# Three more split down projections, three low parts on VectorE, one joint product for router and shared expert

## The chip, the cores and the metric

One core of one Trainium2 chip runs the whole program in one launch. The metric is the device time of one execution in microseconds. The kernel before took 72.2 us in the median of three runs (72.13 to 73.02).

The engines are named as in the profile: PE is TensorE (PEld its weight loads), ACT is ScalarE, DVE is VectorE, POOL is GpSimd and SP is SyncE, which issues almost all transfers.

## The reference, cut to what matters

The input is 4 x 32 tokens of 256 features, so T = 128 tokens, one per partition. Three layers follow one another, each on a layer norm of x and each added to x: a cross attention, a self attention whose four projections carry LoRA updates, and a mixture of experts. The last one is the one that fills the time:

```
logits = flat @ router_w.T                      # 32 experts
scores = sqrt(softplus(logits))
_, idx = top_k(scores + expert_bias, 4)
topv   = take(scores, idx);  topv /= topv.sum() + 1e-20
for every expert e:                             # all 32, weight 0 where not chosen
    g = clip(flat @ wg[e].T, -7, 7); u = clip(flat @ wu[e].T, -7, 7)
    out += p[:, e] * ((silu(g) * u) @ wd[e].T)
out += clamped_swiglu(flat, shared_gate_w, shared_up_w, shared_down_w)
```

Everything is fp32. Each expert has an inner width of 128.

## The kernel before, in words

The experts are taken in 16 pairs, and "unit n" is pair n (n = 1 to 16); unit 0 is the shared expert. In code `p` is the pair counted from 0, so unit n is p = n - 1. For each unit four engines work in turn:

- **PE**, `gate_up(n)` (L581): the product of x with gate and up weights of both experts, 512 columns, into the PSUM bank `bGU[n % 5]`. The first two units (`WHOLE` = 2) are multiplied whole in fp32 (L567). The other units are split: weights and x are each a high part (fp32r) and a low part (the rest), and high times high, high times low and low times high are added, six matmuls a unit.
- **DVE**, `clip(n)` (L955) reads that bank into `gu_clip`; **ACT**, `silu_unit(n)` (L784) writes silu back into the bank; **DVE**, `gate_h(n)` (L1009), two instructions, makes h and so frees the bank (`h_ready`).
- **PE**, `transpose_h(n)` (L593) into `bHT[n % 2]`; **ACT**, `hT_unit(n)` (L790) copies it to SBUF (as a high part for the split downs); **DVE**, `hT_low(n)` (L1022) makes its low part, for split downs only.
- **PE**, `down(n)`: for n up to `FIRST` = 5 in fp32 (L603), and for the last `LAST` = 11 units split (L614, L616).

High parts of weights are copies by ACT (`gu_high` L692 for a pair, `gu_high_chunk` L699 for half a pair, `dn_high` L797 for the down weights of a pair). Low parts are subtractions by POOL: `gu_low(p, c)` (L347), 28 of them, and `dn_low(i)` (L353), 11 of them, where i = 0 is the first split down. POOL does them in a written order: the pairs' gate-up parts one after the other, from p = 12 on (`BETWEEN`) each pair followed by one `dn_low`, and the remaining `dn_low` at the end. The weights come in through eight raw slots and go to seven slots of parts (`SLOTS`), so that ACT's copy for pair p waits until `gate_up` of the unit seven earlier is done.

The order on PE is written out: gate_up(1), the router product (L630) within it, the shared product (L636), gate_up(2) to (5), the transposes of units 0 and 1, and then for n = 2 to 16: gate_up(n + 4), transpose_h(n), down(n - 2) (at n = 2 the shared down, L652). gate_up(n) waits for h_ready of unit n - 5, whose bank it takes. ACT's order in turn n is silu_unit(n + 2), gu_high(10 + n), hT_unit(n), dn_high; DVE's is gate_h(n), clip(n + 2), hT_low(n - 2).

The route from the logits to the expert weights is a chain of small instructions of ACT and DVE (L763 to L998) which starts with an absolute value on ACT (L763). That one waits for the logits and for the third layer norm's 1/sqrt(var) from POOL (`inverse_sqrt(2)`, L329). The DVE clips of units 0 and 1 stand within the chain, those of units 2 and 3 behind gate_h(1).

Earlier, in the self attention, POOL's `inverse_sqrt(1)` (L329) stands behind gu_low(2, 0). It releases the broadcast product L514, then DVE's `xnT` (L922, both halves of the features in one instruction), then the projections of keys and queries (L381).

Of the kernel before, what the change touches and what calls it, by code (L numbers as in the profile page):

```python
# [40 lines left out]
LAST = 11  # L41
BETWEEN = 12
# [13 lines left out]
SMALL = ROUTER + DC * E  # L56
# [14 lines left out]
def build(nc, x, consts, mask, small, ctx_kv, x_wq, lora, rows, attn_w, shared_w, moe_w, out):  # L71
    with ExitStack() as ctx:
# [22 lines left out]
        shared_sb = sb("shared_sb", [128, DC * 2 * I + D])  # L95
# [78 lines left out]
        bLogits, bShared = bXT1, bXT0  # L174
# [4 lines left out]
        bGU = (bP[0][:, 0], bP[0][:, 1], bP[1][:, 0], bP[1][:, 1], bE)  # L179
# [74 lines left out]
        dn_lo_ready = sem("dn_lo_ready")  # L254
        gu_hi_ready = sem("gu_hi_ready")
# [13 lines left out]
        def _(sp):  # L269
# [42 lines left out]
        def _(pool):  # L312
# [43 lines left out]
            for p in range(WHOLE, PAIRS):  # L356
                for c in range(DC):
                    if (p, c) == (WHOLE, 1):
                        inverse_sqrt(1)
# [3 lines left out]
                if p >= BETWEEN:  # L363
                    dn_low(p - BETWEEN)
            for i in range(PAIRS - BETWEEN, LAST):
                dn_low(i)

        @block.tensor
        def _(pe):
# [8 lines left out]
            def project_T(which, c, w, x_t, done, biased=False):  # L378

                for k in range(DC):  # L380
                    last = nc.tensor.matmul(bP[c][:, which, 0:T], w[:, k, c * 128:(c + 1) * 128], x_t[:, k, :],  # L381
# [142 lines left out]
            pe.wait_ge(xn_ready, 1)  # L524
            project_T(0, 0, aw[0], xnT, k_psum, biased=True)
# [70 lines left out]
            def down(n):  # L596
# [49 lines left out]
            for n in range(2, PAIRS + 1):  # L646
# [13 lines left out]
        def _(act):  # L660
# [102 lines left out]
            nc.scalar.activation(abs_logits[:], bLogits[:, 0:E], ACT.Abs, scale=rstd[:, 2:3]).then_inc(abs_ready, 1)  # L763
# [36 lines left out]
            gu_high_chunk(WHOLE + 7, 0)  # L800
            silu_unit(0)
# [20 lines left out]
        def _(dve):  # L822
# [99 lines left out]
            nc.vector.tensor_tensor(xnT[:], xcT[:], bRB.unsqueeze(1).to_broadcast([128, DC, T]), ALU.mult  # L922
# [180 lines left out]
```

## Time and profile before

| | |
|---|---|
| median of 3 runs | 72.2 us |
| time of the profiled execution | 72.16 us |
| its span | 70.3 us |
| busy: PE, ACT, DVE, POOL | 65.7, 46.0, 46.9, 54.0 us |
| granted clock of PE | 0.997 of full |
| transfers | 15.75 MB, done by some 46 us |

The span runs from the first to the last instruction seen by the profile; the rest of the 72.16 us lies around it. Busy time says how full an engine is; the chain that ended last says which engine the end waited for.

### The profile page before, as it was taken

The page shows a single profiled execution, that of the slowest core. Times are in us where ns is not written, and L with a number is a line of the kernel's source. Part 1 is how long each engine was busy: PE and PEld are TensorE (multiplying, and loading weights), DVE is VectorE, ACT ScalarE, POOL GpSimd, SP SyncE. Part 2 cuts the span into 40 slices and gives each one's busy share as a digit, 9 for nine tenths or more (in the row PEclk, how much of TensorE's full clock was granted, in tenths as well). Part 3 has the DMA queues.
Part 4 walks back from the last instruction along what each step waited for, and adds up shares of the span by engine and source line. Part 5 has one row for each costly group of instructions (what it writes and reads, how often), then busy time and mean ns, then how long its engine had stood idle before and what let it go on. Part 6 is the DMA issues. An engine that isn't in the chain of part 4 may idle for free.

```text
span 70.3 us, 1581 instructions
## 1 busy us (share of the span) xinstructions
PE 65.7 (93%) x544; PEld 49.2 (70%) x546; DVE 46.9 (67%) x132; ACT 46.0 (65%) x101; POOL 54.0 (77%) x59
## 2 busy tenths in 40 slices
PE   5999998998998999999999999999999999999940
PEld 2347565787864486648787878888887888788830
DVE  0058489584779536599999907758995887697440
ACT  0604547669988665678989399999968852275220
POOL 6430005499999994999799999999999999999000
PEclk9999999999999999999999999999999999999998
DMA  0899999999999999999999997100000000000002
GB/s 0 261 282 304 343 424 390 235 332 422 429 410 408 389 403 400 403 374 347 384 415 394 396 389 274 54 6 0 0 9 0 0 0 0 0 0 0 5 0 75
DMA packets 6343, 15.75 MB, mean 224 GB/s; under 512 B 704, under 2 KB 1472, under 8 KB 6336
## 3 DMA queue, kind: packets, MB, share of 16 engines
q1 hardware_dynamic: 6048, 15.39, 59.7%
q10 hardware_dynamic: 288, 0.27, 1.1%
q8 instruction: 4, 0.07, 0.4%
q14 instruction: 3, 0.02, 0.1%
HBM read 15.52 MB, written 0.13 MB: 223 GB/s over the span
## 4 chain that ended last, share of the span: by engine, by line
PE 82%; DVE 7%; ACT 4%; POOL 3%; issue 1%
PE bP L581 22%; PE bY L614 7%; PE bY L603 6%; PE bE L444 6%; PE bE L581 6%; PE bXT L593 5%; PE bP L567 5%; PE bP L381 4%; PE bY L616 3%; PE bP L408 2%; DVE shifted L851 2%; POOL gu_w L347 2%; DVE row_max L849 2%; PE bXT L437 1%; ACT probs L669 1%
## 5 line engine op out<-in xcount | busy, mean ns | idle before, releaser
L347 POOL TENSOR_TENSOR gu_w<-gu_raw,gu_w 128x512 fp32r<-128x512 f32 x28 | 35.1, 1287 | 1.4 <-ACT gu_w L699 1.4
L581 PE MATMUL bP<-gu_w,xnT_parts 128*128 128x512 f32 x66 | 18.7, 418 | 0.0
L581 PEld LDWEIGHTS bP<-gu_w,xnT_parts 128*128 128x128 f32 x66 | 12.2, 189 | 3.0 <-issue 0.5
L1009 DVE SCALAR_TENSOR_TENSOR h<-gu_clip,gate,bP 128x128 f32<-128x128 f32 x26 | 7.8, 344 | 5.3 <-ACT bP L784 5.3
L955 DVE TENSOR_SCALAR gu_clip<-bP,clip_at 128x512 f32<-128x512 f32 x13 | 10.4, 806 | 1.1 <-PE bP L581 1.1
L692 ACT ACTIVATE gu_w<-gu_raw 128x1024 fp32r<-128x1024 f32 x9 | 9.4, 1048 | 1.1 <-issue 1.1
L353 POOL TENSOR_TENSOR gu_w<-dn_w,gu_w 128x512 fp32r<-128x512 f32 x8 | 10.0, 1309 | 0.0
L790 ACT ACTIVATE hT_parts<-bXT 128x256 fp32r<-128x256 f32 x11 | 4.2, 384 | 6.4 <-PE bXT L593 6.4
L784 ACT ACTIVATE bP<-gu_clip,rstd 128x256 f32<-128x256 f32 x13 | 6.2, 473 | 0.2 <-DVE gu_clip L955 0.2
L593 PE MATMUL bXT<-consts_sb,h 128*128 128x128 f32 x33 | 6.2, 271 | 0.0
L337 POOL TENSOR_TENSOR aw_sb<-aw_sb,lora_v 128x256 f32<-128x256 f32 x2 | 1.4, 727 | 6.1 <-DMA aw_sb<-attn_w_dram 6.1
L699 ACT ACTIVATE gu_w<-gu_raw 128x512 fp32r<-128x512 f32 x10 | 5.9, 620 | 0.2 <-PE bP L581 0.2
L593 PEld LDWEIGHTS bXT<-consts_sb,h 128*128 128x128 f32 x33 | 4.4, 140 | 1.9 <-DVE h L1009 0.2
L614 PE MATMUL bY<-gu_w,hT_parts 128*128 128x512 f32 x14 | 5.7, 434 | 0.0
L444 PE MATMUL bE<-const-bfloat16-1.0 128*128 128x512 bf16 x12 | 5.0, 566 | 0.8 <-PEq L1096 0.8
L1022 DVE TENSOR_TENSOR hT_parts<-bXT,hT_parts 128x256 fp32r<-128x256 f32 x11 | 4.6, 418 | 1.0 <-ACT hT_parts L790 1.0
L603 PE MATMUL bY<-dn_w,hT 128*128 128x256 f32 x20 | 5.1, 380 | 0.0
L581 PE MATMUL bE<-gu_w,xnT_parts 128*128 128x512 f32 x18 | 4.9, 407 | 0.0
L797 ACT ACTIVATE gu_w<-dn_w 128x512 fp32r<-128x512 f32 x8 | 4.6, 628 | 0.0
L329 POOL TENSOR_TENSOR rstd<-var_eps,inv_sqrt_power 128x1 f32<-128x1 f32 x3 | 1.8, 598 | 2.9 <-DVE var_eps L836 2.9
L567 PE MATMUL bP<-gu_raw,xfT 128*128 128x512 f32 x8 | 4.0, 603 | 0.0
L616 PE MATMUL bY<-gu_w,hT_parts 128*128 128x256 f32 x14 | 3.9, 282 | 0.0
(162 smaller groups left out, 124.3 us busy)
## 6 DMA issues: line engine op xcount, KB each, us to landing
gu_raw<-moe_w_dram SPq DMA_DIRECT2D x16, 512.0 KB, 9.7
dn_w<-moe_w_dram SPq DMA_DIRECT2D x16, 256.0 KB, 9.7
aw_sb<-attn_w_dram SPq DMA_DIRECT2D x2, 512.0 KB, 7.0
shared_sb<-shared_w_dram SPq DMA_DIRECT2D x1, 384.0 KB, 14.5
small_sb<-small_dram SPq DMA_DIRECT2D x1, 370.0 KB, 6.9
xwq_sb<-x_wq_dram SPq DMA_DIRECT2D x1, 256.0 KB, 3.5
lora_sb<-lora_dram SPq DMA_DIRECT2D x1, 256.0 KB, 4.3
ctx_sb<-ctx_kv_dram ACTq DMA_DIRECT2D x1, 192.0 KB, 3.1
```

What stands on the lines that cost most here:

```text
L347: nc.gpsimd.tensor_tensor(gu_w[:, gu_slot(p), 1, cols], gu_raw[:, raw_slot(p), cols], gu_w[:, gu_slot(p), 0, cols], ALU.subtract).then_inc ...
L353: nc.gpsimd.tensor_tensor(dn_parts(i)[:, 1], dn_w[:, at:at + 2 * D], dn_parts(i)[:, 0], ALU.subtract).then_inc(dn_lo_ready, 1)
L444: nc.tensor.matmul(bank, ones, ones_wide, start=True, stop=True, skip_group_check=True)
L567: return nc.tensor.matmul(bGU[n % 5][:, 0:GU], xfT[:, k, :], gu_raw[:, raw_slot(n - 1), k * GU:(k + 1) * GU], start=(k == 0), stop=(k == D ...
L581: last = nc.tensor.matmul(bGU[n % 5][:, 0:GU], xnT_parts[:, a, k, :], gu_w[:, gu_slot(n - 1), w, k * GU:(k + 1) * GU], start=(k == 0 and a ...
L593: last = nc.tensor.transpose(bHT[n % 2][:, e * T:(e + 1) * T], h[:, n % 4, e, :], ident)
L603: last = nc.tensor.matmul(bY[:, 0:D], hT[:, n % 3, e, :], dn_w[:, at:at + D], start=False, stop=False, skip_group_check=True)
L614: nc.tensor.matmul(bY.rearrange("p (w n) -> p w n", w=2), hT_parts[:, n % 3, 0, e, :], parts, start=False, stop=False, skip_group_check=True)
L692: nc.scalar.activation(gu_w[:, gu_slot(p), 0], gu_raw[:, raw_slot(p)], ACT.Copy).then_inc(gu_hi_ready, DC)
L784: nc.scalar.activation(dst, gu_clip[:, n % 4, 0:width, 0, :], ACT.Silu, scale=rstd[:, 2:3]).then_inc(silu_ready, 1)
L955: nc.vector.tensor_scalar(gu_clip[:, n % 4, 0:width], bank[:, 0:width * 2 * I], clip_at[:, 0:1], clip_at[:, 1:2], ALU.min, ALU.max).then_i ...
L1009: last = nc.vector.scalar_tensor_tensor(h[:, n % 4, e], gu_clip[:, n % 4, e, 1, :], weight_e, bank[:, e * 2 * I:e * 2 * I + I], ALU.mult, ...
```

## The change

- `LAST` becomes 14, so `FIRST` is 2: units 3, 4 and 5 have split downs too, 14 in all.
- The low parts of the first three split downs (`STAGED` = 3) are made by DVE: ACT copies the down weights whole into the PSUM bank bE (`dn_stage`), and DVE subtracts the high part from that. POOL makes the other 11. `BETWEEN` becomes 14: POOL makes dn_low(3) behind pair 14, dn_low(4) behind pair 15, and the rest at the end.
- The bank bE is given up by gate_up after unit 4. From unit 6 on four banks are used in turn, and from unit 9 on gate_up(n) waits for h_ready of unit n - 4.
- ACT's order in turn n: silu_unit(n + 2), then (n = 2 to 4) dn_high and dn_stage, hT_unit(n), gu_high(10 + n). dn_stage(0) waits for h of unit 4, each later one for DVE's previous low part.
- Router weights stand behind the shared gate and up weights, in one product of 288 columns, done before the second half of gate_up(1). `gu_ready` counts one less.
- gu_low(2, 0) is made in two halves of 256 columns, with `inverse_sqrt(1)` between them.
- `xnT` is made in two instructions, one for each chunk, and the first projection waits for each chunk by itself.

```diff
-LAST = 11
-BETWEEN = 12
+LAST = 14
+STAGED = 3
+BETWEEN = 14
...
+        bStage = bE
+
+        def bGU(n):
+
+            if n < 6:
+                return (bP[0][:, 0], bP[0][:, 1], bP[1][:, 0], bP[1][:, 1], bE)[n % 5]
+            return (bP[0][:, 1], bP[1][:, 0], bP[1][:, 1], bP[0][:, 0])[(n - 6) % 4]
...
-            for p in range(WHOLE, PAIRS):
+            for half in range(2):
+                cols = slice(half * GU // 2, (half + 1) * GU // 2)
+                pool.wait_ge(gu_hi_ready, 1)
+                low = nc.gpsimd.tensor_tensor(gu_w[:, gu_slot(WHOLE), 1, cols], gu_raw[:, raw_slot(WHOLE), cols],
+                                              gu_w[:, gu_slot(WHOLE), 0, cols], ALU.subtract)
+                if half == 0:
+                    inverse_sqrt(1)
+            low.then_inc(gu_lo_ready[0], 1)
+            gu_low(WHOLE, 1)
+            for p in range(WHOLE + 1, PAIRS):
                 for c in range(DC):
-                    if (p, c) == (WHOLE, 1):
-                        inverse_sqrt(1)
                     if (p, c) == (WHOLE + 5, 0):
                         inverse_sqrt(2)
                     gu_low(p, c)
                 if p >= BETWEEN:
-                    dn_low(p - BETWEEN)
-            for i in range(PAIRS - BETWEEN, LAST):
+                    dn_low(STAGED + p - BETWEEN)
+            for i in range(STAGED + PAIRS - BETWEEN, LAST):
                 dn_low(i)
...
                 if n > 5:
-                    pe.wait_ge(h_ready, n - 4)
+                    pe.wait_ge(h_ready, n - 4 if n < 9 else n - 3)
...
-                    pe.wait_ge(dn_lo_ready, i + 1)
+                    if i < STAGED:
+                        pe.wait_ge(dn_lo_dve_ready, i + 1)
+                    else:
+                        pe.wait_ge(dn_lo_ready, i - STAGED + 1)
...
             pe.wait_ge(xf1_ready, 1)
+            pe.wait_ge(ld["shared"], 16)
             for k in range(DC):
-                last = nc.tensor.matmul(bLogits[:, 0:E], xfT[:, k, :], small_sb[:, ROUTER + k * E:ROUTER + (k + 1) * E],
+                last = nc.tensor.matmul(bShared[:, 0:SHARED], xfT[:, k, :], shared_sb[:, k * SHARED:(k + 1) * SHARED],
                                         start=(k == 0), stop=(k == DC - 1))
             last.then_inc(logits_ready, 1)
             gate_up_whole(1, 1).then_inc(gu_ready, 1)
-            pe.wait_ge(ld["shared"], 16)
-            for k in range(DC):
-                last = nc.tensor.matmul(bShared[:, 0:2 * I], xfT[:, k, :], shared_sb[:, k * 2 * I:(k + 1) * 2 * I],
-                                        start=(k == 0), stop=(k == DC - 1))
-            last.then_inc(gu_ready, 1)
...
+            def dn_stage(i):
+
+                if i:
+                    act.wait_ge(dn_lo_dve_ready, i)
+                else:
+                    act.wait_ge(h_ready, 5)
+                at = (FIRST + i) * 2 * D
+                nc.scalar.activation(bStage[:], dn_w[:, at:at + 2 * D], ACT.Copy).then_inc(stage_ready, 1)
...
                 if n + 2 <= PAIRS:
                     silu_unit(n + 2)
+                if 0 <= n - 2 < STAGED:
+                    dn_high(n - 2)
+                    dn_stage(n - 2)
+                hT_unit(n)
                 if EARLY + n < PAIRS:
                     gu_high(EARLY + n)
-                hT_unit(n)
-                if 0 <= n - 2 < UNITS:
-                    dn_high(n - 2)
...
-            nc.vector.tensor_tensor(xnT[:], xcT[:], bRB.unsqueeze(1).to_broadcast([128, DC, T]), ALU.mult
-                                    ).then_inc(xn_ready, 1)
+            for c in range(DC):
+                nc.vector.tensor_tensor(xnT[:, c], xcT[:, c], bRB, ALU.mult).then_inc(xn_ready, 1)
...
+            def dn_low(i):
+
+                dve.wait_ge(stage_ready, i + 1)
+                dve.wait_ge(dn_hi_ready, i + 1)
+                nc.vector.tensor_tensor(dn_parts(i)[:, 1], bStage[:], dn_parts(i)[:, 0], ALU.subtract
+                                        ).then_inc(dn_lo_dve_ready, 1)
+
             for n in range(2, PAIRS + 1):
                 gate_h(n)
                 if n + 2 <= PAIRS:
                     clip(n + 2)
+                if 0 <= n - 4 < STAGED:
+                    dn_low(n - 4)
                 if n - 2 > FIRST:
                     hT_low(n - 2)
```

## Rows read from the trace of the kernel before

**Rows 1.** Page, busy us of each engine, its share of the span, instructions.
```profile
PE 65.7 (93%) x544; PEld 49.2 (70%) x546; DVE 46.9 (67%) x132; ACT 46.0 (65%) x101; POOL 54.0 (77%) x59
```

**Rows 2.** Chain that ended last, in order: start us, us, what.
```profile
27.86 0.36 PE bXT L630 x4
...
29.17 0.86 PE bXT L636 x4
...
37.68 0.22 PE bXT L593 x2
...
43.31 1.40 PE bE L581 x6
...
44.93 0.86 PE bY L603 x4
...
54.73 0.24 PE bY L614
...
55.44 1.41 PE bE L581 x6
...
66.73 0.13 PE bY L616
```

**Rows 3.** Timeline, 15 to 17 us: start us, us, engine, line, operation, [idle before].
```profile
15.37 0.56 POOL L329 TENSOR_TENSOR rstd<-var_eps,inv_sqrt_power 128x1 f32<-128x1 f32 x1
15.44 0.42 DVE L868 SCALAR_TENSOR_TENSOR aw_sb<-bE,aw_sb 128x256 f32<-128x256 f32 x1
...
15.88 0.29 DVE L918 COPY xcT<-bXT 128x128 f32<-128x128 f32 x1
...
16.56 0.42 DVE L922 TENSOR_TENSOR xnT<-xcT,bE 128x256 f32<-128x256 f32 x1 [0.39 <-PE bE L514]
```

**Rows 4.** Timeline, start of the route's chain.
```profile
27.96 0.68 POOL L329 TENSOR_TENSOR rstd<-var_eps,inv_sqrt_power 128x1 f32<-128x1 f32 x1 [0.96 <-DVE var_eps L836]
...
28.67 0.29 ACT L763 ACTIVATE abs_logits<-bXT,rstd 128x32 f32<-128x32 f32 x1 [1.17 <-POOL rstd L329]
```

**Rows 5.** Timeline, all engines: h of unit 2, silu of unit 3, loads for unit 2's transposes.
```profile
36.80 0.60 DVE L1009 SCALAR_TENSOR_TENSOR h<-gu_clip,gate,bP 128x128 f32<-128x128 f32 x2
36.92 0.48 ACT L784 ACTIVATE bP<-gu_clip,rstd 128x256 f32<-128x256 f32 x1
...
37.45 0.21 PEld L593 LDWEIGHTS bXT<-consts_sb,h 128*128 128x128 f32 x2 [0.21 <-DVE h L1009]
```

**Rows 6.** Timeline of ACT, from pair 12's copy to pair 13's.
```profile
40.10 1.06 ACT L692 ACTIVATE gu_w<-gu_raw 128x1024 fp32r<-128x1024 f32 x1 [1.09 <-issue]
41.07 0.37 ACT L790 ACTIVATE hT<-bXT 128x256 f32<-128x256 f32 x1
41.33 0.62 ACT L797 ACTIVATE dn_first<-dn_w 128x512 fp32r<-128x512 f32 x1
41.85 0.47 ACT L784 ACTIVATE bP<-gu_clip,rstd 128x256 f32<-128x256 f32 x1
42.25 1.04 ACT L692 ACTIVATE gu_w<-gu_raw 128x1024 fp32r<-128x1024 f32 x1
```

**Rows 7.** Timeline of DVE: clip of unit 5, h of unit 4, clip of unit 6.
```profile
38.55 0.81 DVE L955 TENSOR_SCALAR gu_clip<-bP,clip_at 128x512 f32<-128x512 f32 x1
39.27 0.60 DVE L1009 SCALAR_TENSOR_TENSOR h<-gu_clip,gate,bE 128x128 f32<-128x128 f32 x2
39.78 0.81 DVE L955 TENSOR_SCALAR gu_clip<-bP,clip_at 128x512 f32<-128x512 f32 x1
```

**Rows 8.** Groups on DVE by form: busy us, mean ns of one | idle before.
```profile
L844 DVE TENSOR_TENSOR k_heads<-bP,consts_sb 128x512 f32<-128x512 f32 x4 | 2.7, 689 | 1.7 <-PE bP L381 1.0 <-PE bP L455 0.7
...
L1022 DVE TENSOR_TENSOR hT_parts<-bXT,hT_parts 128x256 fp32r<-128x256 f32 x11 | 4.6, 418 | 1.0 <-ACT hT_parts L790 1.0
```

**Rows 9.** Timeline of POOL: its unbroken runs of low parts.
```profile
33.95 10.05 POOL L347 TENSOR_TENSOR gu_w<-gu_raw,gu_w 128x512 fp32r<-128x512 f32 x8 [0.36 <-ACT gu_w L699]
...
55.17 10.04 POOL L353 TENSOR_TENSOR gu_w<-dn_w,gu_w 128x512 fp32r<-128x512 f32 x8
```

More of the change, by code:

```diff
@@ L55 @@
 ROUTER = EBIAS + E
-SMALL = ROUTER + DC * E
+SMALL = ROUTER
+SHARED = 2 * I + E
 def gu_slot(p):
@@ L376, in merge_lora, with project_T @@
                                  start=True, stop=True).then_inc(lora_psum[m], 1)
-            def project_T(which, c, w, x_t, done, biased=False):
+            def project_T(which, c, w, x_t, done, biased=False, chunks_ready=None):
                 for k in range(DC):
+                    if chunks_ready is not None:
+                        pe.wait_ge(chunks_ready, k + 1)
                     last = nc.tensor.matmul(bP[c][:, which, 0:T], w[:, k, c * 128:(c + 1) * 128], x_t[:, k, :],
@@ L522, in values_part @@
                 return values(bE, lambda k: xnT[:, k, :], lambda k: aw[2][:, k, :], DC, batches)
-            pe.wait_ge(xn_ready, 1)
-            project_T(0, 0, aw[0], xnT, k_psum, biased=True)
+            project_T(0, 0, aw[0], xnT, k_psum, biased=True, chunks_ready=xn_ready)
             project_T(1, 0, aw[1], xnT, q_psum)
@@ L580, in gate_up @@
                         for a, w in HI_LO:
-                            last = nc.tensor.matmul(bGU[n % 5][:, 0:GU], xnT_parts[:, a, k, :],
+                            last = nc.tensor.matmul(bGU(n)[:, 0:GU], xnT_parts[:, a, k, :],
                                                     gu_w[:, gu_slot(n - 1), w, k * GU:(k + 1) * GU],
@@ L651, in _ @@
                     pe.wait_ge(ln_step, 3)
-                    nc.tensor.matmul(bY[:, 0:D], hT[:, 0, 0, :], shared_sb[:, DC * 2 * I:], start=False, stop=False,
+                    nc.tensor.matmul(bY[:, 0:D], hT[:, 0, 0, :], shared_sb[:, DC * SHARED:], start=False, stop=False,
                                      skip_group_check=True).then_inc(y_done, 1)
@@ L762, in _ @@
             act.wait_ge(logits_ready, 1)
-            nc.scalar.activation(abs_logits[:], bLogits[:, 0:E], ACT.Abs, scale=rstd[:, 2:3]).then_inc(abs_ready, 1)
+            nc.scalar.activation(abs_logits[:], bLogits, ACT.Abs, scale=rstd[:, 2:3]).then_inc(abs_ready, 1)
             act.wait_ge(abs_ready, 1)
@@ L781, in silu_unit @@
                 width = 2 if n else 1
-                bank = bGU[n % 5] if n else bShared
+                bank = bGU(n) if n else bShared
                 dst = bank[:, 0:width * 2 * I].rearrange("p (e w i) -> p e w i", e=width, w=2)[:, :, 0, :]
@@ L950, in clip @@
                 width = 2 if n else 1
-                bank = bGU[n % 5] if n else bShared
-                dve.wait_ge(gu_ready, max(2, n + 1))
+                bank = bGU(n) if n else bShared
+                if n:
+                    dve.wait_ge(gu_ready, n)
+                else:
+                    dve.wait_ge(logits_ready, 1)
                 if n >= 4:
@@ L966, in _ @@
             dve.wait_ge(abs_ready, 1)
-            step(nc.vector.tensor_scalar(logits_n, bLogits[:, 0:E], rstd[:, 2:3], None, ALU.mult))
+            step(nc.vector.tensor_scalar(logits_n, bLogits, rstd[:, 2:3], None, ALU.mult))
             dve.wait_ge(one_plus_ready, 1)
@@ L1005, in gate_h @@
                     dve.wait_ge(hT_psum, n - 3)
-                bank = bGU[n % 5] if n else bShared
+                bank = bGU(n) if n else bShared
                 for e in range(2 if n else 1):
@@ L1070 @@
     small[:, EBIAS:EBIAS + E] = v["L0_ffn_expert_bias"][None, :]
-    small[:, ROUTER:] = chunked(v["L0_ffn_router_w"]).reshape(128, DC * E)
     w_kv = v["L0_xattn_Wkv_expand"].T
```

20 lines of the change are left out of this document (11 added, 9 removed).

## The prediction

> **What bounds the kernel now.** I read the busy times first. PE is busy for 93% of the span, POOL for 77%, ACT and DVE for two thirds [rows 1]. A share says little over stages, so I took the chain that ended last, in order of time. From the first row of [rows 2] to the last, 27.86 to 66.86 us, it holds PE pieces alone, each beginning where the one before ends. So in that stretch every instruction taken from PE is worth its full length, as long as no wait takes its place. The next question is how near the next wait is. For that I read the timeline around PE's products that depend on h, then ACT's and POOL's queues. Two places are near. The weight loads for the transposes of unit 2 already sat idle for 0.21 us, until DVE ended h of unit 2 at 36.80 + 0.60 = 37.40 us [rows 5]; PE's stream hid that. And POOL makes low parts from 33.95 us, at 10.05 / 8 = 1.256 us each, to 55.17 + 10.04 = 65.21 us [rows 9]; the last split down begins where the chain's last row ends, at 66.86 us [rows 2].
>
> **Early edits, one by one.**
> - Router product: PE loses a piece of 0.36 us; the shared product of 0.86 us grows from 256 to 288 columns, 0.86 x 288 / 256 = 0.97 [rows 2]. Gain 0.25 us.
> - xnT in chunks: one instruction of 0.42 us becomes two; the nearest row with 128 columns takes 0.29 us [rows 3]. The first projection starts 0.13 us earlier, and its first chunk lasts about as long as DVE needs for the second. Gain 0.13.
> - POOL's half low part: 1/sqrt(var) now ends at 15.37 + 0.56 = 15.93 us. Earlier by some 0.2 us, it would no longer be what L514 waits for: DVE's merge ends at 15.44 + 0.42 = 15.86 us [rows 3]. Gain at most 0.07. One more POOL instruction delays later low parts by about half a microsecond; POOL idles 0.96 us before 27.96 us [rows 4], which covers it.
>
> Together PE is 0.45 us earlier at gate_up(2).
>
> **Where that goes.** The route's chain starts with L763 at 28.67 us, when POOL's 1/sqrt(var) ends at 28.64 us [rows 4]. After the change that would be 0.2 us earlier, but the logits now come with the joint product: the router piece ended at 28.22 us, the joint one ends at 27.86 - 0.20 + 0.97 = 28.63 us [rows 2]. So the chain starts when it did. From there DVE is busy almost throughout, up to h of unit 2, which again ends at 37.40 us. The transposes of unit 2 can't start their load before 37.44 us, against 37.45 now [rows 5]. The 0.45 us are spent waiting there. I count the early edits at 0, with bounds of -0.45 (the chain keeps pace) and +0.1 (the logits come later than worked out).
>
> **Three more split downs.** An fp32 down takes 0.86 us [rows 2], a split one 55.44 - 54.73 = 0.71 us [rows 2]. Three of them: -0.45 us, on the path.
>
> **What feeds them, on ACT.** From the starts in [rows 6] each instruction holds ACT for: silu 0.40, copy of a pair 0.97, hT 0.26, down copy 0.52, together 2.15 us a unit, less than the 44.93 + 0.86 - 43.31 = 2.48 us that PE takes [rows 2]. The staging copy has no row. The nearest is the down copy of the same 512 columns, SBUF to SBUF, 0.52 apart and 0.62 long [rows 6]. Lower bound: what 512 more columns cost a copy, 0.97 - 0.52 = 0.45. Upper bound: silu, which writes PSUM, holds ACT 0.14 us longer than hT for as many columns, 256; twice that on 0.52 is 0.80. I take 0.54, near the same shape. Three units then take 2.69 us each, above PE's 2.48.
>
> Walking the new order from silu(3) at 36.92 us [rows 5]: hT(1), pair 11's copy 37.58, silu(4) 38.55, down copy 38.95. dn_stage(0) waits for h of unit 4, which ends at 39.87 us [rows 7], and starts at 39.91. Behind it stand hT(2) and pair 12's copy, which starts at 40.71 us and not at 40.10, where its transfer let it start before [rows 6]. Then, by the same steps: silu(5) 41.68, silu(6) 44.37, pair 14's copy ends 47.14, and the down copy for i = 3 ends at 49.97 us.
>
> The Trainium skill (ScalarE: Activation LUTs, "Step-by-step: what each stage is for") says that ScalarE reaches PSUM faster than SBUF. No row here has the same operation with both targets; by that rule the staging copy lies near its lower bound, and the sum would be +0.3 instead of +0.5 us.
>
> **On DVE.** Three subtractions of 512 columns, one operand in PSUM: 0.69 us each, as L844 [rows 8], and three more hT_low of 0.42. DVE had waited for ACT's silu in these turns, so they fit: the starts are h of unit 5 at 42.19, clip 42.70, subtraction 43.42, hT_low(3) 44.05 (an h holds DVE for 39.78 - 39.27 = 0.51, a clip for 39.27 - 38.55 = 0.72 [rows 7]). hT_low(3) ends at 44.47, in time for PE (43.31 + 1.40 = 44.71 [rows 2]). hT_low(4) ends at 47.16, and with 0.04 for the semaphore and 0.14 for the weight load PE starts at 47.34 instead of 47.07: +0.27 us. The transposes need it because they overwrite its bank. h of units 6 and 7, for which gate_up(10) and (11) wait now that there are four banks, are late by 0.02 and 0.08 us.
>
> **On POOL.** It still makes eleven low parts of downs. But it now waits for ACT's copies: pair 12 at 41.81, pair 13 at 44.49, pair 14 at 47.18, then dn_low(3) at 50.01. Behind that stand two low parts of pair 15 and then dn_low(4), which starts at 50.01 + 3 x 1.256 = 53.78 and ends at 55.07 us. down(7) needs it. It begins at 55.07 + 0.04 + 0.14 = 55.25 us; now it begins at 54.73 [rows 2]. PE would be ready at 54.66, so it waits for 0.59 us. After that POOL gains on PE: its last low part ends near 66.4 us, 0.8 us before it is needed.
>
> **The sum.** 0 (early) - 0.45 + 0.27 + 0.02 + 0.08 + 0.59 = +0.51 us, which is 55.25 - 54.73. On the profiled execution: 72.16 + 0.5 = 72.7 us. That execution stands 0.04 us below the median of 72.2, which I neglect. With the copy at 0.45 the sum is +0.3 (72.5), at 0.80 +1.4 (73.5).
>
> **Rivals.**
> - *The downs' saving stays, the new waits don't.* The early gain is lost at unit 2 all the same. 72.16 - 0.45 = 71.7 us. For it: PE's wait at down(7) is the end of a chain of four small delays, and the instructions in between could be spaced closer. Against it: even with POOL held up only at pair 12, dn_low(4) ends near 54.4 us, and ACT has no idle time left to catch up.
> - *The route's chain comes forward too*, so that 0.45 us early and 0.45 us late both remain: 71.3 us. For it: the joint product might end sooner than by its columns. Against: the idle weight load [rows 5] and the unchanged instructions on DVE.
> - *DVE and POOL block each other*, and it is slower. Each of DVE's three subtractions would hold POOL for its 0.69 us; 2.07 us of delay reach dn_low(4), and down(7) starts at 57.3: 74.7 us. It decides as soon as POOL loses about 0.9 us beyond what I have, for then the total passes 2%. Against it: hT_low, also with one operand in PSUM, takes 0.42 us beside a busy POOL [rows 8], and POOL's parts keep their 1.256 us then [rows 9].
>
> The Trainium skill (SBUF — State Buffer, "SBUF: two separate sides") says that DVE and GpSimd take an exclusive lock when the DVE instruction has two SBUF inputs and GpSimd reads SBUF. By it the staging in PSUM avoids the lock, and this rival falls.
>
> That the change does not do what it says has one form: POOL keeps 11 low parts of downs, so it is relieved of nothing; that is in the forecast.
>
> **Chances.** Forecast 0.62, saving of the downs alone 0.20, both savings 0.08, blocking 0.07, something else 0.03. The range of 71.5 to 73.4 us takes in the first rival and nearly all of the forecast's bounds. 2% is 1.44 us, about what a measurement of this kernel can tell from no change: below 70.8 lies almost nothing, above 73.6 the blocking case. Faster 0.03, same 0.90, slower 0.07.
>
> **What would show it.** L763 starts at 28.6 to 28.7 us although gate_up(2) ends 0.45 us earlier, and PE's loads for the transposes of unit 2 are idle for some 0.6 us. L797 and the staging copy stand ahead of hT in three turns, ACT has no gap between 40 and 50 us. POOL has gaps before pairs 12, 13 and 14 and before dn_low(3). The chain that ended last passes through POOL's dn_low(4) to the down of unit 7 at about 55.2 us. The forecast is wrong if PE has no gap between 44 and 56 us, if h of unit 2 ends before 37.2 us, or if POOL's parts or DVE's subtractions last longer than 1.3 and 0.7 us.

## The result, and the profile after

The changed kernel took 72.87 us (median of 21 runs) beside 72.23 us for the kernel before (21 runs, taken in turn on one chip). The ratio is 1.0092 [1.0065, 1.0119]: 0.66 us more, a real difference, within the 2% that I called no change, and close to the forecast of 72.7. Medians are of all executions; the ratios leave out the slow ones, more than 1.5% above the fastest of their kernel, and the traces of e3, e9, e10 and e12 below are of such (73.91, 73.87, 72.65 and 72.26 us). The profiled execution took 73.24 us, its span 71.4 us; that of before took 72.16 us. So the two traces differ by 1.08 us, 0.4 us more than the ratio says; two waits for transfers that this execution had and most others had not are shown below.

The busy times, page of the changed kernel, against [rows 1]:

```profile
PE 65.5 (92%) x542; PEld 47.8 (67%) x542; DVE 49.9 (70%) x139; ACT 49.1 (69%) x107; POOL 54.5 (76%) x60
```

PE does 0.2 us less in a span that is 1.1 us longer, so PE waited more. ACT and DVE each have 3 us more work, POOL 0.5.

**Two intervals.** The first part of the kernel differs from one execution to the next: the statistics of the third norm start anywhere from 26.20 to 28.86 us in the fourteen traces. To compare kernels all the same, I cut the time at three instructions of DVE: those statistics, the start of h of unit 2, written h(2), and the last addition. Timeline of DVE, kernel before:

```profile
27.04 0.43 DVE L943 BATCH_NORM_STATS2 stats<-bY 128x6 f32<-128x256 f32 x1 [0.52 <-PE bY L433]
...
29.81 0.37 DVE L971 RECIPROCAL bXT<-bXT 128x32 f32<-128x32 f32 x1
...
67.77 0.42 DVE L1037 TENSOR_TENSOR x_sb<-bP,xc 128x256 f32<-128x256 f32 x1
```

and of the changed kernel:

```profile
26.89 0.43 DVE L972 BATCH_NORM_STATS2 stats<-bY 128x6 f32<-128x256 f32 x1 [0.52 <-PE bY L454]
...
30.13 0.37 DVE L1003 RECIPROCAL bXT<-bXT 128x32 f32<-128x32 f32 x1 [0.24 <-DVE bXT L1002]
...
37.13 0.59 DVE L1041 SCALAR_TENSOR_TENSOR h<-gu_clip,gate,bP 128x128 f32<-128x128 f32 x2
...
40.86 0.69 DVE L1061 TENSOR_TENSOR dn_first<-bE,dn_first 128x512 fp32r<-128x512 f32 x1
...
68.87 0.42 DVE L1078 TENSOR_TENSOR x_sb<-bP,xc 128x256 f32<-128x256 f32 x1
```

Interval A, statistics to h(2): 36.80 - 27.04 = 9.76 us before, 37.13 - 26.89 = 10.24 after. Interval B, h(2) to the last addition: 30.97 before, 31.74 after. With the statistics 0.15 us earlier, -0.15 + 0.48 + 0.77 = +1.10 us.

Without one wait the statistics would have come earlier still. From DVE's first read of the key product (`k_heads`) to the statistics it is 27.04 - 17.79 = 9.25 us before, and 9.25 to 9.28 us in eleven of the other traces, but 26.89 - 17.13 = 9.76 us in this one (and 9.84 in e10). ACT's timeline of the changed kernel has a copy there that waited for its transfer, ahead of the queries:

```profile
17.93 0.63 ACT L718 ACTIVATE gu_w<-gu_raw 128x512 fp32r<-128x512 f32 x1 [0.80 <-DMA gu_raw<-moe_w_dram]
```

**Interval B: where PE waited.** The starts of gate_up in PE's timeline show it, for an unhindered unit has a fixed length. Kernel before:

```profile
37.98 1.75 PE L581 MATMUL bP<-gu_w,xnT_parts 128*128 128x512 f32 x6
...
50.43 1.76 PE L581 MATMUL bP<-gu_w,xnT_parts 128*128 128x512 f32 x6
...
52.95 1.56 PE L581 MATMUL bP<-gu_w,xnT_parts 128*128 128x512 f32 x6
...
55.28 1.10 PE L581 MATMUL bE<-gu_w,xnT_parts 128*128 128x512 f32 x4
```

Five units with an fp32 down take (50.43 - 37.98) / 5 = 2.49 us each, the first with a split down 2.52 (it still begins behind an fp32 one), the next 2.33. The changed kernel:

```profile
38.30 1.76 PE L601 MATMUL bP<-gu_w,xnT_parts 128*128 128x512 f32 x6
...
43.34 1.67 PE L601 MATMUL bP<-gu_w,xnT_parts 128*128 128x512 f32 x6
...
46.04 1.63 PE L601 MATMUL bP<-gu_w,xnT_parts 128*128 128x512 f32 x6
...
48.70 1.62 PE L601 MATMUL bP<-gu_w,xnT_parts 128*128 128x512 f32 x6
...
51.08 1.57 PE L601 MATMUL bP<-gu_w,xnT_parts 128*128 128x512 f32 x6
...
53.41 1.57 PE L601 MATMUL bP<-gu_w,xnT_parts 128*128 128x512 f32 x6
...
56.39 1.56 PE L601 MATMUL bP<-gu_w,xnT_parts 128*128 128x512 f32 x6
```

The steps are 2.70, 2.66, 2.38, 2.33, 2.98 us, where without waits they would be 2.52 and then 2.33. So PE waited 0.18, 0.33, 0.05, 0 and 0.65 us. The two steps ahead of them, 43.34 - 38.30 = 5.04 us, are 0.06 longer than twice 2.49: gate_up(9), which now takes the bank of unit 5, started right behind h(5). Waits of 1.27 us less the three downs' saving of 0.48 make 0.79, against the 0.77 of interval B. PE's weight loads show what it waited for:

```profile
37.77 0.20 PEld L613 LDWEIGHTS bXT<-consts_sb,h 128*128 128x128 f32 x2 [0.55 <-DVE h L1041]
...
45.05 0.20 PEld L613 LDWEIGHTS bXT<-consts_sb,h 128*128 128x128 f32 x2 [0.48 <-issue]
...
47.71 0.20 PEld L613 LDWEIGHTS bXT<-consts_sb,h 128*128 128x128 f32 x2 [0.48 <-issue]
...
55.58 0.19 PEld L637 LDWEIGHTS bY<-gu_w,hT_parts 128*128 128x128 f32 x1 [0.62 <-POOL gu_w L365]
```

The first answers to the load in [rows 5]: idle 0.55 us instead of 0.21. The next two are the transposes of units 5 and 6, whose bank DVE has to have read first. The profile names no releaser, but they start 0.11 and 0.12 us behind the ends of hT_low(3) and hT_low(4) in DVE's timeline, and h and ACT's copy of that bank were done 1 us and more ahead of the loads:

```profile
44.53 0.41 DVE L1054 TENSOR_TENSOR hT_parts<-bXT,hT_parts 128x256 fp32r<-128x256 f32 x1
...
47.18 0.41 DVE L1054 TENSOR_TENSOR hT_parts<-bXT,hT_parts 128x256 fp32r<-128x256 f32 x1
```

The last is down(7), for POOL. POOL's timeline answers to [rows 9]:

```profile
34.05 7.54 POOL L359 TENSOR_TENSOR gu_w<-gu_raw,gu_w 128x512 fp32r<-128x512 f32 x6 [0.59 <-ACT gu_w L718]
42.37 7.86 POOL L359 TENSOR_TENSOR gu_w<-gu_raw,gu_w 128x512 fp32r<-128x512 f32 x6 [0.78 <-ACT gu_w L711]
50.48 1.29 POOL L365 TENSOR_TENSOR gu_w<-dn_w,gu_w 128x512 fp32r<-128x512 f32 x1 [0.26 <-ACT gu_w L816]
...
54.25 12.56 POOL L365 TENSOR_TENSOR gu_w<-dn_w,gu_w 128x512 fp32r<-128x512 f32 x10
```

The unbroken run that began at 33.95 in [rows 9] is now cut at pairs 12, 13, 14 and before dn_low(3): by 0.78, by 0.32 together for pairs 13 and 14 (7.86 - 7.54, six parts each), and by 0.26 us, 1.36 us in all. dn_low(4) starts at 54.25 us, and the chain that ended last passes through it:

```profile
50.48 1.29 POOL gu_w L365
51.77 2.51 POOL gu_w L359 x2
54.28 1.25 POOL gu_w L365
55.58 0.50 PE bY L637
```

From there to 67.97 us it holds PE alone. ACT's timeline, against [rows 6]:

```profile
40.22 0.60 ACT L827 ACTIVATE bE<-dn_w 128x512 f32<-128x512 f32 x1 [0.34 <-DVE h L1041]
40.76 0.37 ACT L809 ACTIVATE hT<-bXT 128x256 f32<-128x256 f32 x1
41.23 1.06 ACT L711 ACTIVATE gu_w<-gu_raw 128x1024 fp32r<-128x1024 f32 x1
42.19 0.46 ACT L803 ACTIVATE bP<-gu_clip,rstd 128x256 f32<-128x256 f32 x1
...
43.11 0.58 ACT L827 ACTIVATE bE<-dn_w 128x512 f32<-128x512 f32 x1
43.63 0.36 ACT L809 ACTIVATE hT_parts<-bXT 128x256 fp32r<-128x256 f32 x1
...
44.84 0.46 ACT L803 ACTIVATE bP<-gu_clip,rstd 128x256 f32<-128x256 f32 x1
```

The staging copy holds ACT for 40.76 - 40.22 = 0.54 us, the next for 0.52, and silu(5) to silu(6) takes 44.84 - 42.19 = 2.65 us (walked: 2.69). hT to pair 12's copy takes 0.47 us instead of 0.26. The copy waits for two things only, its transfer and gate_up(6), which was done before 38.30 us, so here it was the transfer: ACT's queue stood at that wait (L710) for 0.95 us, and for 0.04 us in a second trace of this kernel (e11). That is the 0.2 us by which interval B exceeds that of e11.

### The profile page after: what moved, and what is told of

The parts are those of the page before. It is cut to its first block, busy times and chain, and to the rows that moved or that the text cites. A ratio compares the mean times of both kernels' runs of the same rounds, so it can differ in the third digit from the quotient of the medians.

```text
span 71.4 us, 1596 instructions
## 1 busy us (share of the span) xinstructions
PE 65.5 (92%) x542; PEld 47.8 (67%) x542; DVE 49.9 (70%) x139; ACT 49.1 (69%) x107; POOL 54.5 (76%) x60
## 4 chain that ended last, share of the span: by engine, by line
DMA 30%; PE 25%; POOL 13%; ACT 12%; SPq 8%; DVE 5%; issue 3%; ACTq 0%
DMA gu_raw<-moe_w_dram 30%; POOL gu_w L359 9%; PE bY L637 6%; PE bP L601 6%; SPq L285 4%; POOL gu_w L365 4%; PE bY L639 3%; ACT gu_w L711 2%; PE bXT L613 2%; SPq L293 2%; ACT bP L803 2%; ACT hT_parts L809 2%; PE bP L429 2%; ACT bE L827 2%; PE bXT L458 1%
## 5 line engine op out<-in xcount | busy, mean ns | idle before, releaser
L359 POOL TENSOR_TENSOR gu_w<-gu_raw,gu_w 128x512 fp32r<-128x512 f32 x27 | 33.9, 1285 | 1.6 <-ACT gu_w L711 0.8
L601 PE MATMUL bP<-gu_w,xnT_parts 128*128 128x512 f32 x78 | 21.4, 410 | 0.0
L601 PEld LDWEIGHTS bP<-gu_w,xnT_parts 128*128 128x128 f32 x78 | 14.0, 188 | 3.6 <-issue 0.5
L365 POOL TENSOR_TENSOR gu_w<-dn_w,gu_w 128x512 fp32r<-128x512 f32 x11 | 13.8, 1296 | 0.3 <-ACT gu_w L816 0.3
L987 DVE TENSOR_SCALAR gu_clip<-bP,clip_at 128x512 f32<-128x512 f32 x15 | 12.0, 804 | 0.5 <-PE bP L601 0.5
L1041 DVE SCALAR_TENSOR_TENSOR h<-gu_clip,gate,bP 128x128 f32<-128x128 f32 x30 | 9.0, 343 | 3.8 <-ACT bP L803 3.7
L637 PE MATMUL bY<-gu_w,hT_parts 128*128 128x512 f32 x20 | 8.2, 436 | 0.4 <-POOL gu_w L365 0.4
L816 ACT ACTIVATE gu_w<-dn_w 128x512 fp32r<-128x512 f32 x11 | 6.4, 630 | 0.0
L639 PE MATMUL bY<-gu_w,hT_parts 128*128 128x256 f32 x20 | 5.6, 281 | 0.0
L637 PEld LDWEIGHTS bY<-gu_w,hT_parts 128*128 128x128 f32 x20 | 3.8, 188 | 1.1 <-POOL gu_w L365 0.6
L639 PEld LDWEIGHTS bY<-gu_w,hT_parts 128*128 128x128 f32 x20 | 3.8, 189 | 0.0
```

Of the source, the lines that this page charges most:

```text
L359: nc.gpsimd.tensor_tensor(gu_w[:, gu_slot(p), 1, cols], gu_raw[:, raw_slot(p), cols], gu_w[:, gu_slot(p), 0, cols], ALU.subtract).then_inc ...
L365: nc.gpsimd.tensor_tensor(dn_parts(i)[:, 1], dn_w[:, at:at + 2 * D], dn_parts(i)[:, 0], ALU.subtract).then_inc(dn_lo_ready, 1)
L601: last = nc.tensor.matmul(bGU(n)[:, 0:GU], xnT_parts[:, a, k, :], gu_w[:, gu_slot(n - 1), w, k * GU:(k + 1) * GU], start=(k == 0 and a == ...
L637: nc.tensor.matmul(bY.rearrange("p (w n) -> p w n", w=2), hT_parts[:, n % 3, 0, e, :], parts, start=False, stop=False, skip_group_check=True)
L639: last = nc.tensor.matmul(bY[:, 0:D], hT_parts[:, n % 3, 1, e, :], parts[:, 0], start=False, stop=False, skip_group_check=True)
L816: nc.scalar.activation(dn_parts(i)[:, 0], dn_w[:, p * 2 * D:(p + 1) * 2 * D], ACT.Copy).then_inc(dn_hi_ready, 1)
```

## The experiments

Each kernel was compared with the kernel before on the same chip, e1 to e4 on one, e5 to e8 on a second, e9 to e12 on a third. A and B are the two intervals, in us, from each kernel's trace; A + B leaves out what happens ahead of the statistics. e5, e6, e8, e9 and e10 leave out parts of the route and don't compute the reference.

| kernel | A | B | A + B | ratio |
|---|---|---|---|---|
| before | 9.76 | 30.97 | 40.73 | |
| changed | 10.24 | 31.74 | 41.98 | 1.0092 [1.0065, 1.0119] |
| e1_pool_order | 10.24 | 30.89 | 41.13 | 1.0041 [0.9993, 1.0088] |
| e2_early_only | 10.24 | 30.92 | 41.16 | 1.0022 [0.998, 1.0064] |
| e3_late_only | 9.97 | 31.53 | 41.50 | 1.0125 [1.005, 1.0199] |
| e4_no_stage | 10.28 | 31.80 | 42.08 | 1.0214 [1.014, 1.0287] |
| e5_before_short | 9.58 | 31.06 | 40.64 | 1.003 [0.9982, 1.0077] |
| e6_early_short | 9.86 | 30.92 | 40.78 | 1.0018 [0.9968, 1.0067] |
| e7_spread | 10.23 | 30.48 | 40.71 | 1.0001 [0.996, 1.0042] |
| e8_spread_short | 9.82 | 30.36 | 40.18 | 0.9897 [0.9852, 0.9943] |
| e9_before_fast | 9.16 | 31.46 | 40.62 | 1.0006 [0.9959, 1.0052] |
| e10_early_fast | 9.82 | 31.68 | 41.50 | 1.0008 [0.9951, 1.0064] |
| e11_after_again | 10.23 | 31.53 | 41.76 | 1.0127 [1.0051, 1.0202] |
| e12_spread_router | 9.98 | 30.36 | 40.34 | 0.9938 [0.9884, 0.9992] |

### e1: is it POOL's order?

```
-                if p >= BETWEEN:
-                    dn_low(STAGED + p - BETWEEN)
-            for i in range(STAGED + PAIRS - BETWEEN, LAST):
+                if p == BETWEEN:
+                    dn_low(STAGED)
+                    dn_low(STAGED + 1)
+            for i in range(STAGED + 2, LAST):
```

> The changed kernel with one difference: POOL makes dn_low(3) and dn_low(4) both behind pair 14, ahead of pair 15. Theory (down(7) waits for dn_low(4), which stands behind two low parts of pair 15): dn_low(4) ends two parts, 2.5 us, earlier, PE's wait at down(7) goes, and the time falls by 0.6 us against the changed kernel, to about that of the kernel before (within 0.2 us). Rival (the wait is only where PE's lateness shows, which comes from the transfers of the gate-up weights and ACT's queue): the time stays as that of the changed kernel, +0.6 us.

Measured: 1.0041. POOL's timeline has both parts together, ahead of pair 15:

```profile
49.95 2.54 POOL L365 TENSOR_TENSOR gu_w<-dn_w,gu_w 128x512 fp32r<-128x512 f32 x2 [0.24 <-ACT gu_w L817]
```

PE has no wait at down(7): gate_up(7) to gate_up(14) takes 17.23 us (before 17.30, changed 18.09, e11 17.86), and B is 0.64 us under e11's. So the wait goes as soon as the two parts of pair 15 no longer stand ahead of dn_low(4), though ACT's copies are as late as in the changed kernel. That doesn't clear ACT: the order costs something only because POOL had already lost 1.36 us to those copies. Without these, by my estimate, dn_low(4) ends at 55.54 - 1.36 = 54.18 us in the old order, and down(7) could not start its loads before 55.58 - 0.62 = 54.96. By that the wait needed both. Against the kernel before, e1 is at +0.30 us [-0.05, +0.63], and A + B at +0.40, where I had expected at most 0.2: what is left is interval A.

### e2 and e3: the two halves of the change

e2 keeps the joint router product, xnT in chunks and the half low parts, and takes back the late part; e3 the reverse.

```
e2:  -LAST = 14  +LAST = 11     -STAGED = 3  +STAGED = 0     -BETWEEN = 14  +BETWEEN = 12
     five banks for gate_up as before; pe.wait_ge(h_ready, n - 4)
e3:  -SHARED = 2 * I + E  +SHARED = 2 * I     router product by itself, in bXT1
     no halves of pair 2's low part; xnT in one instruction
```

> The kernel before with the early edits alone: joint product of router and shared expert, gu_low(2, 0) in two halves, xnT in two chunks. 11 split downs and five banks as before. Theory (the 0.45 us that PE gains by gate_up(2) are spent waiting for h of unit 2): same time as before, -0.1 to +0.1 us. Rival (the gain is kept): -0.45 us.

> The changed kernel without the early edits: router product by itself, gu_low(2, 0) and xnT whole. Theory (the end is set by POOL's dn_low(4), which the early edits don't reach): same time as the changed kernel, +0.5 to +0.7 us against before. Rival (the joint product, which holds up the logits, is what costs): about -0.3 to 0 us against before.

e2 measured 1.0022, that is +0.16 us with an interval of 0.3 on either side: no gain is seen, and the -0.45 us of the rival is excluded. The weight loads of PE for the transposes of unit 2 are idle as in the changed kernel:

```profile
37.38 0.20 PEld L611 LDWEIGHTS bXT<-consts_sb,h 128*128 128x128 f32 x2 [0.55 <-DVE h L1038]
```

e3 measured 1.0125, +0.9 us [+0.4, +1.4]: the late part alone costs about as much as the whole. PE's timeline has the wait at down(7):

```profile
56.23 0.50 PE L630 MATMUL bY<-gu_w,hT_parts 128*128 128x512 f32 x1 [0.40 <-POOL gu_w L365]
```

B is 30.97 + 0.56, where the walk said +0.51.

### e4: what the staging in PSUM buys

```
-                    dn_high(n - 2)
-                    dn_stage(n - 2)
+                    dn_high(n - 2)
 ...
-                nc.vector.tensor_tensor(dn_parts(i)[:, 1], bStage[:], dn_parts(i)[:, 0], ALU.subtract
+                nc.vector.tensor_tensor(dn_parts(i)[:, 1], dn_w[:, at:at + 2 * D], dn_parts(i)[:, 0], ALU.subtract
```

> The changed kernel without the three staging copies: DVE subtracts the high part from the down weights in SBUF, so both its operands lie in SBUF. Theory (the three copies of 0.54 us on ACT are what delays silu and POOL's copies): ACT's queue is 1.6 us shorter, no wait arises at units 5 to 7, -0.5 us against before, if DVE and POOL don't block each other. Rival (DVE and POOL block each other when DVE reads two operands from SBUF): each of DVE's three subtractions lasts up to 1.3 us longer than 0.69, or POOL's part beside it does, and the time is that of before or above it.

Measured: 1.0214, slower than the changed kernel though ACT has three copies less. By how much is open: 0.9 us by this ratio and 1.0092, 0.6 us by this one and e11's 1.0127, 0.1 and 0.3 us by A + B. DVE's timeline:

```profile
41.38 1.31 DVE L1060 TENSOR_TENSOR dn_first<-dn_w,dn_first 128x512 fp32r<-128x512 f32 x1
...
43.86 1.78 DVE L1060 TENSOR_TENSOR dn_first<-dn_w,dn_first 128x512 fp32r<-128x512 f32 x1
...
47.13 1.46 DVE L1060 TENSOR_TENSOR dn_first<-dn_w,dn_first 128x512 fp32r<-128x512 f32 x1
```

and POOL's:

```profile
34.60 16.40 POOL L359 TENSOR_TENSOR gu_w<-gu_raw,gu_w 128x512 fp32r<-128x512 f32 x12 [0.64 <-ACT gu_w L718]
...
42.10 1.74 POOL L359 TENSOR_TENSOR gu_w<-gu_raw,gu_w 128x512 fp32r<-128x512 f32 x1
...
45.05 1.72 POOL L359 TENSOR_TENSOR gu_w<-gu_raw,gu_w 128x512 fp32r<-128x512 f32 x1
```

The same subtraction takes 0.69 us with one operand in PSUM and 1.31 to 1.78 us with both in SBUF; POOL's parts take 16.40 / 12 = 1.367 us on average instead of 1.256, so it lost 1.3 us (the first row holds all twelve, the others two of them alone). The ends show how the two engines kept each other from SBUF. The subtraction of 43.86 us ends at 45.64. POOL's part before ends as the next begins, at 45.05 to 45.09: the subtraction stood until then and did its work in the 0.55 us left. POOL's next part stood for those 0.5 us, and took 1.72. The Trainium skill (SBUF — State Buffer, "SBUF: two separate sides") states such a lock for a DVE instruction with two SBUF inputs; this trace agrees. The mechanism of my third rival exists, at a lower price than I gave it; the staging is what keeps the changed kernel clear of it, where the subtraction takes 0.68 to 0.69 us.

### e5 and e6: a shorter route

Both leave out, in the route, the copy of the left-over, the top-8 search and the replacement, so that h comes earlier; e5 in the kernel before, e6 in e2. Every expert then keeps a weight.

```
-            step(nc.vector.tensor_copy(score2[:, E:E + 1], leftover[:]))
 ...
-            step(nc.vector.max(top8[:], key[:]))
-            step(nc.vector.match_replace(replaced[:], top8[:], key[:], -SENTINEL))
 ...
```

> The kernel before with a shorter route: a copy, the top-8 search and the match-replace are left out, so every expert gets its weight and the choice of four isn't made. DVE's chain up to h of unit 2 is some 0.7 us shorter. Theory (PE's stream alone sets the end, h of unit 2 just in time): no change against before, -0.1 to +0.1 us. Rival (the route's chain already bounds the kernel before): faster by 0.2 us or more.

> The early edits alone (as in e2) and the shorter route of e5, without the choice of four experts. Theory (the early gain is lost only in the wait for h of unit 2): h of unit 2 ends 0.7 us earlier, the wait is gone, and the 0.45 us reach the end: -0.35 to -0.45 us against e5 and against before. Rival (there never was a gain on PE, or another wait takes it): same as e2.

e5: A shrank by only 0.18 us, for h(0) then waited 0.21 us for ACT's silu, which is right behind; the 0.7 us I had expected was wrong. The end came 0.09 us earlier (A + B), nothing in the times. e6: the loads for unit 2 still sat idle for 0.55 us,

```profile
36.72 0.20 PEld L611 LDWEIGHTS bXT<-consts_sb,h 128*128 128x128 f32 x2 [0.55 <-DVE h L1035]
```

so the wait wasn't removed, against what I had expected. But against e2 h(2) came 0.38 us sooner after the statistics and A + B fell by 0.38 us, one to one; in the kernel before half of the smaller step of 0.18 us was lost. The ratios, 1.003 and 1.0018, can't tell the two apart.

### e9 and e10: a route shorter still

They also leave out the second reciprocal and the product behind it, and ACT does silu(0) and silu(1) ahead of a half of pair 9.

```
-            step(nc.vector.reciprocal(inv_root, root[:]))
-            step(nc.vector.tensor_tensor(inv_root, inv_root, softplus[:], ALU.mult))
-            gu_high_chunk(WHOLE + 7, 0)
             silu_unit(0)
             silu_unit(1)
+            gu_high_chunk(WHOLE + 7, 0)
```

> The kernel before with a much shorter way to h of unit 2, on both engines: on DVE the route leaves out the copy, the top-8 search, the match-replace, and the reciprocal and product behind the root (neither the choice of four nor the scores are the reference's); on ACT silu of units 0 and 1 stand ahead of the first half of pair 9's copy. Theory (PE's stream alone sets the end of the kernel before): the time stays that of before, within 0.1 us, though h of unit 2 ends a microsecond earlier. Rival (the way to h of unit 2 bounds it too): faster by 0.3 us or more.

> The early edits alone with the same shorter way to h of unit 2 as e9, the same parts of the route left out. Theory (the early gain is lost in that wait and nowhere else): the weight loads for the transposes of unit 2 have no wait, the stretch from the third norm's statistics to the last addition is 0.25 us shorter than in e9 (the joint product), and the time 0.3 to 0.45 us less than e9's. Rival (another wait takes it): same as e9, and loads for the transposes idle again.

e9: h(2) came 0.60 us sooner (of the microsecond expected), the end 0.11 (A 9.16, B 31.46), and no change is seen in the time, within 0.3 us. PE's stream stayed where it was: gate_up(7) starts 39.78 - 28.86 = 10.92 us behind the statistics, before 37.98 - 27.04 = 10.94. So in the kernel before DVE's chain to h(2) doesn't bound. e10 failed as a test. Its addition, which had one operand in PSUM, now had two in SBUF beside a busy POOL:

```profile
32.38 1.07 DVE L1016 TENSOR_TENSOR bXT<-softplus,root 128x32 f32<-128x32 f32 x1
```

POOL's part that ran then, from 32.10 to 33.40 us, ends 0.05 us before the addition does. e9 has the same addition with the same operands:

```profile
33.89 0.33 DVE L987 TENSOR_TENSOR bXT<-softplus,root 128x32 f32<-128x32 f32 x1
```

It came late in POOL's part (32.88 to 34.16 us), and ended 0.06 us behind that one. That chance of the timing took 0.74 us from e10, and in this trace ACT also sat idle for 2.27 us ahead of pair 12's copy, its queue standing at the wait for the transfer (L708, 3.08 us). With both, neither this trace nor 1.0008 says anything on the theory.

### e7, e8 and e12: the same work, spread

e7 keeps 14 split downs and three low parts on DVE, but for i = 0, 3 and 5 instead of 0, 1 and 2, so that ACT's staging copies don't stand in three turns running, and POOL takes i = 1, 2 behind pair 12 and i = 4 behind pair 14. e8 adds the shorter route. e12 is e7 with the router product by itself.

```
-STAGED = 3
-BETWEEN = 14
+STAGED = (0, 3, 5)
+POOL_LOW = {12: (1, 2), 14: (4,), 15: (6, 7, 8, 9, 10, 11, 12, 13)}
 ...
-                if p >= BETWEEN:
-                    dn_low(STAGED + p - BETWEEN)
+                for i in POOL_LOW.get(p, ()):
+                    dn_low(i)
```

> The changed kernel with DVE's three low parts spread: i = 0, 3 and 5 in place of 0, 1 and 2, so ACT stages in turns 2, 6 and 7 and not in 2, 3 and 4; POOL makes 1 and 2 behind pair 12, 4 behind pair 14 and the other eight behind pair 15. Theory (three staging copies in a row make ACT late, and POOL's order makes PE wait): by the walk no wait is left at units 5 to 7 nor at down(7), so the downs' saving of 0.45 us is kept: -0.5 us against before, -1.1 against the changed kernel. Rival (a split down fed by staging costs as much as it saves wherever it stands): 0 to +0.6 us against before.

> The spread kernel of e7 with the shorter route of e5, without the choice of four experts. Theory (two waits took both gains, and both are gone here): early 0.45 and late 0.45 reach the end together, -0.9 us against e5 and against before. Rival (only one of the two is real): -0.5 us.

> The spread kernel of e7 with the router product by itself, as before the change. Theory (the joint product holds the logits back, and PE waits for h of unit 2 anyway): ACT's first step of the route starts when POOL's 1/sqrt(var) is there, 0.2 us earlier against the third norm's statistics, and PE's extra 0.25 us lie in the wait: -0.1 us against e7. Rival (PE's stream counts in full): +0.25 us against e7.

e7: 1.0001, that is 0.9% under the changed kernel. PE and its loads have no wait from 40 us on, and B is 30.48, 0.49 us under that of before, which is three downs' saving. It is 0.41 under e1's, where PE had kept the waits behind hT_low (0.42 in e11): POOL's order took away the one kind of wait, the spread staging the other. POOL's timeline:

```profile
41.60 2.53 POOL L360 TENSOR_TENSOR gu_w<-gu_raw,gu_w 128x512 fp32r<-128x512 f32 x2 [0.57 <-ACT gu_w L710]
44.09 2.55 POOL L366 TENSOR_TENSOR dn_first<-dn_w,dn_first 128x512 fp32r<-128x512 f32 x2
46.60 5.07 POOL L360 TENSOR_TENSOR gu_w<-gu_raw,gu_w 128x512 fp32r<-128x512 f32 x4
```

After pair 12 it never waits. But against the kernel before I had expected -0.5 us and the ratio shows none, within 0.3 us: A is 0.47 us longer, and that ate the saving in A + B. e8: 0.9897, -0.75 us where -0.9 was expected; against e7 h(2) comes 0.41 us sooner and A + B is 0.53 less. So once the waits behind it are gone, DVE's chain to h(2) sets the time.

e12: A is 0.25 us shorter than e7's. The route's start on ACT:

```profile
29.21 0.29 ACT L785 ACTIVATE abs_logits<-bXT,rstd 128x32 f32<-128x32 f32 x1 [1.17 <-POOL rstd L342]
```

It waits for POOL again, as in [rows 4], not for PE. Ratio 0.9938 [0.9884, 0.9992], medians 72.05 and 72.49: the one version that computes the reference and is faster than the kernel before, by some 0.4 us, though the interval all but reaches 1. The traces agree: A + B is 40.34, against 40.73. Over e7 I had expected 0.1 us; A + B is 0.37 less, 0.25 of it in A. The ratios of the two can't be told apart, but the rival's +0.25 us is not seen.

### e11: the changed kernel again

Nothing is edited; the run asks whether the late reciprocal and the 0.77 us of interval B were chance.

> The changed kernel again, on the chip of this call. Theory: +0.6 us against before, a wait of PE at down(7) of 0.4 us and more, hT_low the last thing before the transposes of units 5 and 6. The reciprocal that stands behind the route's first sum on DVE will or will not start 0.25 us late as in the first trace; if it always does, it belongs to this program and not to chance.

The reciprocal's delay came back in DVE's timeline,

```profile
30.19 0.37 DVE L1003 RECIPROCAL bXT<-bXT 128x32 f32<-128x32 f32 x1 [0.25 <-DVE bXT L1002]
```

so it belongs to the program. B was 31.53, +0.56; here pair 12's copy followed hT at 0.26 us. PE's waits by the starts of gate_up were 0.05, 0.32, 0.05, 0 and 0.65 us. So 0.2 us of the 0.77 was a transfer of that one execution.

## Why the prediction was right, by its steps

- **PE alone bounds the kernel before.** Right: e9, h(2) 0.60 us sooner, 0.11 gained.
- **Early edits lost at unit 2.** Right in kind (e2: +0.16 [-0.14, +0.46] us; loads idle 0.55 us, "some 0.6" forecast). I said that the route would start when it did before; it started at 28.78, 0.1 us later than before, and 1.89 - 1.63 = 0.26 us later behind the statistics, which is the joint product (e12 takes exactly that back). The fault is in what I set against it: DVE's chain I took as unchanged, and its reciprocal starts 0.24 us late. So A grew by 0.48 us. The statistics' earlier start, 0.15 us in the changed kernel's trace and 0.56 in e2's, pays that back in part or whole: h(2) came at 37.13 and 36.72 us, against 36.80 before. The term that I set at 0, with +0.1 as its bound, measured +0.33 and -0.08; the bound was too tight. That the median still came within 0.2 us of the forecast is in part luck: one cost was missing from the sum, and how early the statistics came hid much of it.
- **The xnT chunks and the half low part.** The second merge to the first chunk took 16.02 - 15.01 = 1.01 us, before 16.56 - 15.44 = 1.12: 0.11 us, of at most 0.07 forecast. From there to DVE's first read of the key product it took 17.13 - 16.02 = 1.11 us, before 17.79 - 16.56 = 1.23: 0.12 us, of 0.13 forecast. Both bring the statistics forward, and the route starts behind these, so the 0.23 us aren't lost: they pay half of the 0.48 that A grew by. The rest, 0.25 us, less 0.05 in B, is what e2 (+0.16) should then cost.
- **Three split downs, -0.45.** 2.49 - 2.33 = 0.16 each: -0.48.
- **ACT.** Staging copy 0.54 taken, 0.52 to 0.54 measured, 0.58 to 0.60 long beside 0.61 to 0.62 for the copy SBUF to SBUF. The Trainium skill (ScalarE: Activation LUTs, "Step-by-step: what each stage is for") says that ScalarE is faster into PSUM. These rows show it by 0.02 us only, and the two copies also differ in what they write (f32 and fp32r); the spacing gains nothing, and the lower bound of 0.45 that I had tied to that rule was not reached.
- **DVE.** Subtractions 0.68 to 0.69, as forecast from [rows 8]. Waits of PE behind it: forecast 0.27 + 0.02 + 0.08 = 0.37, measured 0.42 in e11 (0.05, 0.32, 0.05) and 0.62 in the changed kernel's trace (0.06, 0.18, 0.33, 0.05), 0.2 of it pair 12's transfer.
- **POOL, +0.59 at down(7).** Measured 0.65; e1 removes it whole. Starts in the walk came 0.3 to 0.5 us late, 0.33 of it from h(2) and most of the rest from the transfer: dn_low(4) 53.78 walked, 54.25 found; the weight load of down(7) 55.11 and 55.58. Too low was the price of the restart: from that load to gate_up(14) the chain has 56.55 - 55.58 = 0.97 us, where a down in an unbroken stream has 0.71, so 0.26 us, and not the 0.14 of a weight load.
- **Sum of interval B.** Forecast +0.51; e3 and e11 +0.56.
- **Rivals.** Saving without waits: false here, but e7 shows that it needed only another order. Route brought forward: false. Blocking: false for this kernel; as soon as the operand in PSUM is gone it is there (e4), but POOL lost 1.3 us to it and not 2.07.

**Open.** Why the reciprocal starts late: the changed kernel and all kernels built from it have it, e3 too, and before, e5 and e9 don't. I know of no edit that they share and that touches this instruction, and no run isolates it; its 0.22 us of interval A are therefore found and not explained. And no run took DVE's chain wholly off PE's path in an early version; that it binds there rests on e2 to e6 and e7 to e8, where the end moved as h(2) did.

## What to carry to other kernels

Before you move work off the engine that bounds, list what its helpers hand over in order, and find the first item whose place in the queue now comes too late; here two parts, placed ahead of one that was due sooner on an engine that was already late, cost 0.65 us, more than the 0.48 that the three cheaper products gained. Spread added work over turns that have slack instead of putting it into three in a row (e7). And when one engine alone bounds, a second chain may lie only some 0.2 us behind it ([rows 5]): merging two small products to save the first engine 0.25 us cost the second 0.26.

## What the runs showed of the hardware

- A DVE subtraction of 512 columns took 0.69 us with one operand in PSUM, and 1.31 to 1.78 us with both in SBUF beside a busy POOL (e4). Each of the three ends 0.54 to 0.55 us after POOL's instruction of the moment, and POOL's next takes 1.72 to 1.74 us instead of 1.28. A small one pays by where it falls: two additions of 32 columns ended 0.05 to 0.06 us after POOL's, 0.33 and 1.07 us after their own start (e9, e10).
- An instruction may start 0.24 to 0.26 us behind its own engine's previous one in one program and 0.03 us behind it in another: the reciprocal, in all eleven traces of the changed kernel and its variants, in none of the three of before, e5 and e9.
- ACT's copy of 512 columns costs the same spacing into PSUM and into SBUF: 0.52 to 0.54 us.
- PE's restart behind a wait cost more than its weight load: 0.97 us from the load of down(7) to the next gate_up, against 0.71 in an unbroken stream.
